# A graph network's first gathers: four pairs of edge groups instead of two take rows of x, with source columns loaded directly

## What is computed

```
# layer 0 (x: 6250x128, src/dst: 100000, edge_feat: 100000x16)
msg_input = concat([h[src], h[dst], edge_feat])            # 272 columns
messages  = silu(msg_input @ W1 + b1) @ W2 + b2
agg       = segment_sum(messages, dst)
h_new     = silu(concat([h, agg]) @ W3 + b3) @ W4 + b4
x1        = layernorm(x + h_new + h)
# layer 1
agg = segment_sum(x1[src], dst)
z   = relu(((1 + eps) * x1 + agg) @ V1 + c1) @ V2 + c2
out = layernorm(x1 + relu(layernorm(z + x1) * gamma + beta))
```

## Time and profile before

| | |
|---|---|
| Device time, median of 3 runs | 1891.93 us (1882.76 to 1894.49) |
| Span of the profiled execution | 1500.6 us |
| What lies around the span, the median against the span | 391.3 us |
| PE busy | 1285.9 us, 86% |
| POOL busy | 1107.0 us, 74% |
| DVE busy | 1014.5 us, 68% |
| ScalarE (ACT) busy | 642.1 us, 43% |

### The profile page before, as it was taken

The page is one execution under the profiler, slowest core; times in us unless marked ns, Lnnn a source line. Parts: engine busy times, 40 slices in busy tenths (PEclk is TensorE's granted clock), DMA queues, the critical chain, the costliest instruction groups (busy, mean ns, idle before and its releaser), DMA issues.

```text
span 1500.6 us, 31339 instructions
## 1 busy us (share of the span) xinstructions
PE 1285.9 (86%) x8165; PEld 1063.6 (71%) x8165; DVE 1014.5 (68%) x2310; ACT 642.1 (43%) x1257; POOL 1107.0 (74%) x1164
## 2 busy tenths in 40 slices
PE   6788789778777889888888888885999999999992
PEld 6666667556556667767767776764899999998982
DVE  4678888677665565665566656643666888878866
ACT  2744556555555555555556555551111111111111
POOL 5777777777777777777777777777777777777771
PEclk9898889999998999999999999997999999999996
DMA  6533333333336454454455445433887778778731
GB/s 206 135 85 92 93 95 94 95 96 91 95 90 119 118 138 125 126 136 131 125 131 133 125 128 135 113 80 105 258 261 230 208 230 241 222 230 241 213 92 47
DMA packets 189124, 214.15 MB, mean 143 GB/s; under 512 B 60426, under 2 KB 149517, under 8 KB 189011
## 3 DMA queue, kind: packets, MB, share of 16 engines
q1 hardware_dynamic: 138399, 131.62, 28.9%
q0 software_dynamic: 36352, 74.52, 21.3%
q10 hardware_dynamic: 14260, 6.68, 1.6%
HBM read 202.74 MB, written 9.85 MB: 142 GB/s over the span
## 4 chain that ended last, share of the span: by engine, by line
POOL 42%; PE 32%; issue 15%; DVE 4%; DMA 4%; SPq 1%; ACT 1%; DVEq 0%; ACTq 0%; POOLq 0%
POOL gath L873 42%; PE bank L1434 9%; PE bank L1410 8%; PE bank L1362 4%; DMA gath<-src_term,src_col 2%; PE bank L1240 2%; PE bank L1250 2%; PE bank L1233 2%; PE bank L1421 1%; DMA T<-in_x 1%; DMA gath<-layer_input,src_col 1%; PE bank L1396 1%; PE bank L1383 1%; PE bank L1441 0%; PE bank L1456 0%
## 5 line engine op out<-in xcount | busy, mean ns | idle before, releaser
L873 POOL DMA_INDIRECT gath<-src_term,src_col x768 | 737.2, 960 | 234.2 <-issue 230.2
L873 POOL DMA_INDIRECT gath<-layer_input,src_col x336 | 329.6, 981 | 105.6 <-issue 100.6
L1240 PE MATMUL bank<-gath,ident 128*128 128x512 f32 x384 | 218.3, 652 | 114.5 <-DMA gath<-src_term,src_col 113.8
L1233 PEld LDWEIGHTS bank<-terms_r,terms_l 128*128 128x128 f32 x1568 | 209.4, 201 | 83.1 <-issue 69.2
L1233 PE MATMUL bank<-terms_r,terms_l 128*128 128x128 f32 x1568 | 219.6, 286 | 30.4 <-ACT msg L1022 22.0
L1923 DVE TENSOR_SCALAR_CACHE_REDUCE terms_l<-dst_bc,node_col 64x512 f32<-64x512 int32 x196 | 221.0, 1128 | 13.1 <-issue 7.2
L1250 PEld LDWEIGHTS bank<-oh,msg 128*128 128x128 f32 x1568 | 198.7, 202 | 26.9 <-issue 26.1
L1934 DVE TENSOR_TENSOR S<-S,bank 128x128 f32 x98 | 28.1, 286 | 270.2 <-PE bank L1252 178.2
L1250 PE MATMUL bank<-oh,msg 128*128 128x128 f32 x1568 | 202.3, 285 | 0.0
L1434 PE MATMUL bank<-S 128*128 128x288 f32 x672 | 170.0, 406 | 0.1
L1649 DVE TENSOR_TENSOR oh<-bank,dst_rel 128x1024 f32<-128x1024 f32 x140 | 169.8, 1213 | 0.0
(11 more groups left out here) (219 smaller groups left out, 1754.7 us busy)
## 6 DMA issues: line engine op xcount, KB each, us to landing
dst_bc<-in_dst SPq DMA_DIRECT2D x195, 128.0 KB
xT<-sorted_src SPq DMA_DIRECT2D x42, 512.0 KB
xs<-layer_input SPq DMA_DIRECT2D x136, 128.0 KB
gath<-src_term,src_col POOLq DMA_INDIRECT x768
terms_l<-layer_input SPq DMA_DIRECT2D x88, 128.0 KB
terms_r<-layer_input SPq DMA_DIRECT2D x88, 128.0 KB
msg<-layer_input SPq DMA_DIRECT2D x80, 128.0 KB
ef_s<-in_edge_attr SPq DMA_DIRECT2D x97, 64.0 KB
```

Source lines behind the costliest of these rows:

```text
L873: g.indirect_dma_start(out=to[:, j * D:(j + 1) * D], out_offset=None, in_=table[0:rows, :], in_offset=bass.IndirectOffsetOnAxis(ap=indices ...
L1233: mm(bank[h][:, j * D:(j + 1) * D], terms_l[:, u, h, j, :], terms_r[:, u, h, j, :], start=j == 0, stop=False)
L1240: mm(bank[h][:, :], ident[:, :], gath[:, slot, :], start=False, stop=True).then_inc(pre_ps, 1)
```

## The change

`FROM_X` goes from 2 to 4: the first eight groups gather rows of x. Their source indices come as columns from a new DMA, the first that SP issues, in pieces of 4 indices (16 B), into `first_src`; the other groups' columns are made as before, and POOL waits for them before pair 4. The first eight groups keep their turned rows in their own buffers, so that the ring is free for groups 8 to 15, which wait for the turning of an earlier group instead of an addition. The four products for the edge features' weights go from POOL to ScalarE, as 16 activations in steps 7 to 10 of the blocks. The weights' product moves one step later on PE and DVE. Two memsets of POOL go ahead of the identity. Six semaphores become three.

```
-FROM_X = 2
+FROM_X = 4
...
+        first_src = sb("first_src", [P, 2 * FROM_X, CH], I32)
+        from_x_more = sb("from_x_more", [P, 2 * FROM_X - 4, CH * D])
...
@@ SP
+            sp.dma_start(first_src[:, :, :], src[0:2 * FROM_X * GE].rearrange("(g p j) -> p g j", p=P, j=CH)) \
+                .then_inc(first_src_in, 16)
             for blocks_of, to_in in zip(X_BLOCKS, x_in):
...
@@ POOL
+            g.memset(cdeg[:, :], 0.0)
+            g.memset(no_dst[:, :], int(PAD_DST))
             pool.wait_ge(id_zero, 1)
             g.affine_select(out=ident[:, :], ...
-            g.memset(cdeg[:, :], 0.0)
-            g.memset(no_dst[:, :], int(PAD_DST))
-
-            pool.wait_ge(own_rows_made, 1)
-            pool.wait_ge(wef_in, 16)
-            for u in range(2):
-                for h in range(2):
-                    shape = [P, CH, D]
-                    g.tensor_tensor(terms_r[:, u, h, :, :], wef[:, :].unsqueeze(1).to_broadcast(shape),
-                                    own_rows[:, h * CH:(h + 1) * CH].unsqueeze(2).to_broadcast(shape),
-                                    ALU.mult).then_inc(wef_ready, 1)
...
+                if k == 0:
+                    pool.wait_ge(first_src_in, 16)
                 if k == FROM_X:
+                    pool.wait_ge(cols_ready, OF_SRC)
                     source_table_stored()
                 for g in (2 * k, 2 * k + 1):
                     if k < FROM_X:
-                        gather_rows(x, N, g, src_col[:, g * CH:(g + 1) * CH], gathered[g], from_x[g])
+                        gather_rows(x, N, g, first_src[:, g, :], gathered[g], from_x[g])
                         continue
-                    if g >= RING:
+                    if g >= 2 * FROM_X + RING:
                         pool.wait_ge(pre_ps, done(g - RING))
+                    else:
+                        pool.wait_ge(from_x_turned, g - RING + 1)
                     gather_rows(A_d, N, g % RING, src_col[:, g * CH:(g + 1) * CH], gathered[g % RING])
...
-            pool.wait_ge(src_ready, 1)
             skewed(NPAIR + BRIDGED, [(0, gather_sources), (9, rsqrt0_of)])
...
@@ ScalarE
+            def edge_weights(u, h):
+
+                if u == 0 and h == 0:
+                    act.wait_ge(own_rows_made, 1)
+                    act.wait_ge(wef_in, 16)
+                for j in range(CH):
+                    c = h * CH + j
+                    last = a.activation(terms_r[:, u, h, j, :], wef[:, :], ACT.Copy, scale=own_rows[:, c:c + 1])
+                last.then_inc(wef_ready, 1)
+
+            blocks((0, keep_x), (0, only_at({7 + 2 * u + h: lambda u=u, h=h: edge_weights(u, h)
+                                             for u in range(2) for h in range(2)})))
-            blocks((0, keep_x))
...
@@ PE, add_from_x
-                    mm(ps[:, j * D:(j + 1) * D], gath[:, g, j * P:(j + 1) * P], wab[:, 0:D], start=False, stop=False)
+                    mm(ps[:, j * D:(j + 1) * D], from_x[g][:, j * P:(j + 1) * P], wab[:, 0:D], start=False, stop=False)
...
@@ PE, steps
-                  at_steps({4: weight_products, **{k + 1: lambda k=k: turn_from_x(k) for k in range(FROM_X)}}),
+                  at_steps({FROM_X + 1: weight_products, **{k + 1: lambda k=k: turn_from_x(k) for k in range(FROM_X)}}),
...
@@ DVE
-                    ve_.tensor_copy(gath[:, g, :], bank[5 + h][:, :]).then_inc(from_x_kept, 1)
+                    ve_.tensor_copy(from_x[g], bank[5 + h][:, :]).then_inc(from_x_kept, 1)
...
-                5: weight_products, **{k + 2: lambda k=k: keep_from_x(k) for k in range(FROM_X)}}), *in_banks(9, rows0),
+                FROM_X + 2: weight_products, **{k + 2: lambda k=k: keep_from_x(k) for k in range(FROM_X)}}), *in_banks(9, rows0),
```

More of the change, by code:

```diff
@@ L245, in build @@
         sums_early_ps = bank[6][:, P:P + DW]
-        from_x = [xs[:, h, :, :].rearrange("p t d -> p (t d)") for h in range(2)] + [xTs[:, h, :] for h in range(2)]
+        from_x = [xs[:, h, :, :].rearrange("p t d -> p (t d)") for h in range(2)] + [xTs[:, h, :] for h in range(2)] + \
+            [from_x_more[:, h, :] for h in range(2 * FROM_X - 4)]
         x1_rows = As[:, 0, :, :].rearrange("p (s t) d -> p s t d", s=2)
@@ L280, in build @@
         wef_ready = sem("wef_ready")
[L281 to L286, removed]
+        first_src_in = sem("first_src_in")
+        rows_prep = sem("rows_prep")
+        rows_turned = sem("rows_turned")
+        cols_ready = sem("cols_ready")
+        OF_SRC, OF_DST = 1, 2
         lo_made = sem("lo_made")
@@ L1132, in _, with turn_rows @@
             mm = nc.tensor.matmul
[L1134 to L1138, removed]
+            def turn_rows(rows_f, of):
+                pe.wait_ge(rows_prep, of)
+                if of > 1:
+                    pe.wait_ge(cols_ready, of - 1)
                 for q, n in ((0, P), (1, GT)):
@@ L1143, in turn_rows @@
                             rows_f[0:n, q, :].rearrange("g (p j) -> g j p", j=CH)[:, j, :], ident[0:n, 0:n])
-                last.then_inc(turned, 1)
+                last.then_inc(rows_turned, 1)
             pe.wait_ge(consts, 1)
@@ L1176, in _ @@
             blocks((0, turn_x), (1, terms), (0, only_at({
-                6: lambda: turn_rows(src_rows_f, src_prep, None, src_turned), 10: spread_bases})))
-            turn_rows(dst_rows_f, dst_prep, src_ready, dst_turned)
+                6: lambda: turn_rows(src_rows_f, OF_SRC), 10: spread_bases})))
+            turn_rows(dst_rows_f, OF_DST)
             pe.wait_ge(A_made, done(NB))
-            pe.wait_ge(dst_ready, 1)
+            pe.wait_ge(cols_ready, 2)
             pe.wait_ge(base_ready, 1)
@@ L1512, in any_order @@
                 all_units1(pe, hidden1, out1)
-            steps(pe, NPAIR - 2, (4,) + TURNS + tuple(s + 1 for s in TURNS) + (SORTED, SORTED + 1),
+            steps(pe, NPAIR - 2, (FROM_X + 1,) + TURNS + tuple(s + 1 for s in TURNS) + (SORTED, SORTED + 1),
                   of_early(3, early_kept), of_pair(1, turn_ef), of_pair(2, pre_sums), of_early(3, early_sums),
@@ L1526, in _, with cols_of @@
             ve_ = nc.vector
-            def cols_of(turned, column, last_p):
-                dve.wait_ge(turned, 1)
+            def cols_of(of, column, last_p):
+                dve.wait_ge(rows_turned, of)
                 for q, g0, n in ((0, 0, P), (1, P, GT - 1)):
@@ L1536, in cols_of, with to_float @@
                 return ve_.tensor_copy(column[0:last_p, (NG - 1) * CH:NG * CH], ps[0:last_p, n, :])
-            def to_float(rows, rows_f, landed, made):
+            def to_float(rows, rows_f, landed):
                 dve.wait_ge(landed, 16 * 4)
                 ve_.tensor_copy(rows_f[:, 0, :], rows[:, 0, :])
-                ve_.tensor_copy(rows_f[0:GT, 1, :], rows[0:GT, 1, :]).then_inc(made, 1)
+                ve_.tensor_copy(rows_f[0:GT, 1, :], rows[0:GT, 1, :]).then_inc(rows_prep, 1)
             def keep_A(b, u, t, nt):
@@ L1557, in least_dst @@
             def least_dst():
-                dve.wait_ge(dst_prep, 1)
+                dve.wait_ge(rows_prep, OF_DST)
                 ve_.tensor_reduce(lo[:, 0:1], dst_rows_f[:, 0, :], AX_X, ALU.min)
@@ L1590, in find_misfits @@
             def find_misfits():
-                dve.wait_ge(dst_ready, 1)
+                dve.wait_ge(cols_ready, OF_DST)
                 ve_.tensor_tensor(past[:, :].rearrange("p (g j) -> p g j", j=CH),
@@ L1622, in _ @@
             blocks((1, keep_A), (1, order_xT), (0, only_at({
-                4: lambda: to_float(src_rows, src_rows_f, src_in, src_prep),
-                6: lambda: cols_of(src_turned, src_col, P).then_inc(src_ready, 1),
-                7: lambda: to_float(dst_rows, dst_rows_f, dst_in, dst_prep), 8: least_dst, 9: diagonals,
+                4: lambda: to_float(src_rows, src_rows_f, src_in),
+                6: lambda: cols_of(OF_SRC, src_col, P).then_inc(cols_ready, 1),
+                7: lambda: to_float(dst_rows, dst_rows_f, dst_in), 8: least_dst, 9: diagonals,
                 11: window_bases})))
-            cols_of(dst_turned, dst_col, LAST_P).then_inc(dst_ready, 1)
+            cols_of(OF_DST, dst_col, LAST_P).then_inc(cols_ready, 1)
             relative_dst()
-            dve.wait_ge(src_ready, 1)
+            dve.wait_ge(cols_ready, 2)
             ve_.tensor_copy(iota_ps, iota_w[:, 0:PW]).then_inc(iota_kept, 1)
```

## The result

The changed kernel takes 1912.87 us (median of 7 runs, 1911.05 to 1920.14) where the kernel before takes 1891.93 (7 runs, 1882.76 to 1903.7): ratio 1.0098, 95% interval 1.0072 to 1.0123. I forecast 1888 and 1875 to 1899.

What follows compares the result with a forecast made beforehand. POOL's gather stream was taken to bound layer 0: a 16.7 us head start, cut to 6.1 by the ring, less 2.5 for delayed loads, won 3.6. Span 1497.0 with the 391.3 left unchanged gave 1888 us, range 1875 to 1899.

Steps and rivals of the forecast that it cites:

- lies 391.3 above the profiled span: Whole kernel: the median 1891.93 exceeds the 1500.6 us span by 391.3 us, left unchanged when forecasting the time.
- In layer 0 POOL is the clock.: Layer 0: POOL's 768 gathers of A set the pace, losing about 2 us in 970.
- ring bound of 6.1: Before group 16: eight slots make its gather wait for group 8's addition at 97.8, leaving 6.1 us won.
- Head start: 16.7 us.: Start of POOL's gathers: first at about 6.4 us, group 8's at 46.8 instead of 63.5.
- no cost: Gathers of groups 8 to 15: waiting for PE's turning of groups 1 to 8 instead of additions costs nothing.
- The ring: Eight slots of gathered groups: a new POOL wait on PE of 8 to 12 us before group 16.
- 1.79 us more, 3.58 per pair.: PE, pairs 2 and 3: turning, product and b1, less the identity product, add 1.79 us per group.
- 109.2 us of waits: PE, 250 to 1000 us: its waits for gathered rows would later take up the compute's lag.
- The small load: First DMA on SP, 1,024 pieces of 16 B: taken as 5.5 us, between 3.2 and 12.8.
- d: Delay of the loads of x by the work added ahead: 2.5 us taken, bounds 0 and 5.2.
- Edge weights: ScalarE's 16 activations: 4.3 us in four parts of 1.1, cost 0, at most 1.1 us more delay.
- The slower rival: SP's queue: small pieces block the loads of x for 22.9 us, giving 1909 us; chance 0.16.

Runs made afterwards that it cites:

- h3: The changed kernel with POOL waiting, ahead of each layer 0 group, until the previous group's four gathers have landed; 1980.9 us, ratio 1.0232 to the kernel before.
- h1: The kernel before with POOL waiting, ahead of each layer 0 group, until the previous group's four gathers have landed; 2004.49 us, ratio 1.0354.
- f3: The kernel before with FROM_X = 4 alone, so four pairs take rows of x; ratio 1.0072.
- f1: The kernel before with only the new first DMA of index columns added, which nobody reads; ratio 0.999.
- e1: The kernel before, unchanged, profiled again; profiled execution 1889.32 us, ratio 0.9981.
- f2: The kernel before with only the edge weights' rows moved from POOL's products to 16 ScalarE activations; ratio 1.0025.
- g2: The changed kernel with FROM_X = 2 and, right behind its early gathers, 16 more gathers of x that nobody reads; ratio 1.0186 to the kernel before.
- g1: The changed kernel, with POOL issuing the gathers of pairs 2 and 3 only once all of A is stored; ratio 1.012 to the kernel before.
- h5: g2 with its 16 unread gathers paced, each four after the previous four have landed; ratio 1.0125 to the kernel before.
- i2: The changed kernel with h3's waits in groups 1 to 15 and, in all later groups of both layers, a short pause behind the first gather; ratio 0.9938.

## Why the prediction was wrong

- **"The median ... lies 391.3 above the profiled span; I leave that as it is."** This is the step that failed, and all others rest on it. Around the span lie 1.9 us. The 389 were in the walk and the second layer of another kind of execution, in which the holds are missing. I carried a gain of 3.6 us from an execution in which POOL sets the pace over to executions in which the stalled walk does.
- **"In layer 0 POOL is the clock."** True in the trace, false in the timed runs (152.2 us of POOL's waits on PE's additions against 4.0). Where POOL was made the clock, the change won 23.6 us (h3 to h1), so the head start is real, and with 13.7 us at group 16 larger than my ring bound of 6.1 allowed.
- **"Head start: 16.7 us."** The first gather is at 4.02, not 6.4; group 8 at 71.16, not 46.8. The wait for PE's turning (of groups 0 to 7, not 1 to 8), "no cost", cost POOL 36.8 us in four waits, because the walk's first product was at 67.98. For 32 x gathers in a row, which stall what must turn them, I had no term.
- **The ring.** The wait before group 16 is where I put it, 13.51 us against 8 to 12. It came late but as told: w2t is at 128.03, not near 91, and group 8's addition follows it.
- **"1.79 us more, 3.58 per pair."** I misread a row: turns are recorded once, not twice like the products, so the x8 of line 1211 in the earlier trace rows is both groups of a pair. By these rows it is 0.44 + 0.89 + 0.89 - 0.86 = 1.36 us a group, 2.7 a pair. Measured were 4.5 (f3 to f1), and on a walk that nothing covers. The "109.2 us of waits" that were to take up the lag do not occur in e1: PE never waits for gathered rows of A there.
- **The small load.** 5.5 us taken until its columns are there; it was issued at 0.86 and landed 2.2 us later. For d 2.5 us were taken; f1, the load alone, shows none.
- **Edge weights.** Four parts of 1.28 us against 1.1; f2 can't tell their cost from nothing.
- **The slower rival** had a fitting time (1909) and the wrong mechanism. The mechanism of the lost start, POOL's own unbroken train stalling the engines, was in none of my cases. Four pairs doubled the train of x gathers from 16 to 32. It can account for the 12.4 us of group 16, not for what comes behind group 120.

## To carry to other kernels

Compare the span of a profiled execution with the timed runs first: where they differed by 391 us here, the trace showed another regime, and no bound read from it held. Engines that idle with nothing to wait for, in patches that end when POOL pauses, may be paying for long runs of indirect gathers, as here; lengthening these then costs time even where no engine waits for them (g2). Try a real pause between groups where POOL has room for it, and check in the trace that the patches went.

## What was unexpected of the hardware

- In executions like the timed ones PE slows to an instruction each 0.7 to 3.5 us some 8 us into an unbroken run of indirect gathers (e1, g1, h5, i2), and in runs of 32 and more PE and ScalarE can stand for 12 to 24 us (changed kernel, g2, g4).
- In the execution of 1500.6 us much longer runs do nothing of the kind: from 22.5 us to the end of layer 0 no pause of POOL between gathers is over 0.32 us, and PE's waits with the name "issue" are 8.9 us over the span. What differs between the executions isn't known. The granted clock is higher there (0.945 to 0.877); whether that is cause or effect isn't shown.
- Instruction loads in the DMA queues: in the changed kernel none is recorded between 13.7 and 50.9 us, while e1 has one at 23.4. The Trainium skill, Runtime: NRT & Kernel Launch, Instruction fetch mechanics, says that each engine's sequencer fetches its next block by a DMA queue of its own while it runs the present one. A late load would fit, but an engine that stands still also asks for none, and the load at 50.9 comes after ScalarE and PE have gone on (49.15, 49.83), so it did not release them. No row here shows what did.
